# Perceiver kernel on one core: order of the folded queries at the head, and filler matmuls at three places

## The reference

```python
x = x + _L0_xattn_ref(_layernorm(x), ctx_768, Wq, Wk, Wv, Wo, bo)      # 8 heads of 64
x = x + _L0_attn_ref(_layernorm(x), ...)                               # 16 heads of 16, masked
x = x + _L0_ffn_ref(_layernorm(x), ...)                                # 16 experts, top 2, capacity 20 a expert, and a shared one
x = x + _L1_xattn_ref(_layernorm(x), ctx_768, ctx_768, ...)            # 16 heads of 16
x = x + _L1_attn_ref(_layernorm(x), ...)                               # linear attention and a feed-forward part
x = x + _L1_ffn_ref(_layernorm(x), ...)                                # 8 experts, each takes its 32 best tokens
```

```python
q = (x @ Wq).reshape(B, Nq, H, D)
k = (context @ Wk).reshape(B, Nkv, H, D)
v = (context @ Wv).reshape(B, Nkv, H, D)
sim = jnp.einsum('bihd,bjhd->bhij', q, k) * SCALE
attn = jax.nn.softmax(sim, axis=-1)
out = jnp.einsum('bhij,bjhd->bihd', attn, v).reshape(B, Nq, H * D)
return out @ Wo + bo
```

## Time and profile before

| | us |
|---|---|
| median of 3 runs | 1153.56 |
| lowest and highest | 1152.36 and 1153.65 |
| the profiled execution's own time | 1152.36 |
| its span in the profile | 1150.6 |
| TensorE's mean granted clock | 0.984 |
| TensorE busy (matmuls) | 1112.0, 97% of the span |
| VectorE busy | 653.5, 57% |
| ScalarE busy | 665.7, 58% |
| GpSimd busy | 218.8, 19% |

### The profile page before, as it was taken

How to read it: one execution, slowest core, us unless ns; L and a number is a source line. 1 busy time by engine, 2 the same in 40 slices (tenths; PEclk the granted TensorE clock), 3 DMA queues, 4 the chain that set the end, 5 groups by cost and what they waited for, 6 DMA issues and landing times.

```text
span 1150.6 us, 28454 instructions
## 1 busy us (share of the span) xinstructions
PE 1112.0 (97%) x9902; PEld 919.3 (80%) x9902; DVE 653.5 (57%) x1107; ACT 665.7 (58%) x1102; POOL 218.8 (19%) x316
## 2 busy tenths in 40 slices
PE   6999899999999999999987999999999999999998
PEld 4788688888888888888863788888887888888874
DVE  4999654444444444444364688888886444444342
ACT  1888343343433433434231488887888999999631
POOL 0000100000000000000003477777770110000030
PEclk8999899999999999999999999999999999999988
DMA  3544620101110011100445477667665897655191
GB/s 133 136 138 136 248 82 29 35 27 27 29 34 27 27 28 36 27 27 19 169 178 215 136 232 236 219 227 227 225 223 191 307 311 250 199 183 196 63 399 42
DMA packets 63577, 163.28 MB, mean 142 GB/s; under 512 B 6912, under 2 KB 8384, under 8 KB 58368
## 3 DMA queue, kind: packets, MB, share of 16 engines
q1 hardware_dynamic: 54592, 119.06, 32.2%
q0 software_dynamic: 8960, 43.87, 10.0%
HBM read 124.08 MB, written 38.80 MB: 142 GB/s over the span
## 4 chain that ended last, share of the span: by engine, by line
PE 86%; DVE 7%; issue 5%; DMA 1%; DVEq 1%; ACT 1%; POOL 0%; ACTq 0%
PE ps L707 55%; PE ps L957 8%; PE ps L891 8%; PE ps L695 2%; PE ps L742 2%; DVE wide L1456 1%; DVE wide L1464 1%; PE ps L753 1%; PE ps L757 1%; PE ps L754 1%; PE ps L755 1%; PE ps L756 1%; PE ps L1108 1%; PE ps L1279 1%; DMA wa<-ex_in 1%
## 5 line engine op out<-in xcount | busy, mean ns | idle before, releaser
L1526 DVE TENSOR_TENSOR wide<-wide,probs 128x1024 f32<-128x1024 f32 x97 | 118.9, 1226 | 225.3 <-ACT probs L549 224.9
L1456 DVE TENSOR_TENSOR wide<-ps,wide 128x512 f32<-128x512 f32 (+1 forms) x194 | 185.7, 957 | 28.2 <-PE ps L707 23.8
L534 ACT CAST wide<-ps 128x512 bf16<-128x512 f32 x294 | 161.9, 586 | 30.7 <-PE ps L707 25.7
L549 ACT ACTIVATE probs<-ps 128x512 f32<-128x512 f32 x196 | 114.7, 599 | 81.2 <-PE ps L707 81.2
L707 PE MATMUL ps<-q_ha,t_ha 128*128 128x512 f32 x392 | 157.5, 402 | 4.0 <-DVE q_le L1386 3.8
L559 ACT ACTIVATE probs<-ps 128x1024 f32<-128x1024 f32 x132 | 128.0, 1026 | 17.5 <-PE ps L707 15.5
L1464 DVE TENSOR_TENSOR wide<-wide 128x512 bf16<-128x512 bf16 (+1 forms) x194 | 108.0, 557 | 13.0 <-ACT wide L534 2.6
L707 PE MATMUL ps<-q_ab,q_hk 128*128 128x512 f32 x392 | 107.6, 395 | 1.4 <-DVE q_ab L1392 1.3
L707 PEld LDWEIGHTS ps<-q_ha,t_ha 128*128 128x128 f32 x392 | 75.7, 193 | 22.3 <-DVE q_le L1386 4.3
L544 ACT COPY weights_q<-ps 128x512 f32<-128x512 f32 x48 | 28.1, 586 | 106.0 <-PE ps L891 90.0
L1514 DVE COPY v_sb<-wide 128x256 f32<-128x256 f32 x98 | 28.7, 295 | 98.7 <-PE ps L957 97.9
(11 more groups left out here) (421 smaller groups left out, 2400.3 us busy)
## 6 DMA issues: line engine op xcount, KB each, us to landing
raw<-ctx_in SPq DMA_DIRECT2D x147, 256.0 KB, 2.7
k_mem<-q_hk SPq DMA_DIRECT2D x49, 512.0 KB, 3.0
v_mem<-probs SPq DMA_DIRECT2D x49, 256.0 KB, 3.4
wide<-v_mem SPq DMA_DIRECT2D x49, 256.0 KB, 4.0
q_le<-k_mem SPq DMA_DIRECT2D x17, 512.0 KB, 4.3
q_ab<-k_mem SPq DMA_DIRECT2D x16, 512.0 KB, 4.0
q_hk<-k_mem SPq DMA_DIRECT2D x16, 512.0 KB, 4.1
ring<-ex_in POOLq DMA_DIRECT2D x5, 1152.0 KB, 13.3
```

The lines of the kernel that those rows point to most:

```text
L534: act.copy(half16[:, c:c + 512], ps[:, back_bank(layer, q) + u, :]).then_inc(sem(f"half{layer}"), 1)
L549: act.activation(e_keep[GT * slot + j][:, u * 512:(u + 1) * 512], ps[:, s_bank[j][u], :], ACT.Exp).then_inc(sem("exp0"), 1)
L1456: dve.tensor_tensor(r, scores, r, ALU.max).then_inc(sem(f"front{layer}"), 1)
L1526: dve.tensor_tensor(run[:, 0:1024], run[:, 0:1024], e, ALU.add).then_inc(sem("lsum"), 1)
```

## The change

1. The weights' load is cut at another column: the key weights (1284 columns, 657 KB) come alone, with a semaphore of their own (`wk0_loaded`), and value and output weights (2304 columns, 1180 KB) are loaded after the first two context groups. VectorE waits for them after pass 1.
2. The scaling of the queries is gone; the scale is in the mask that the block diagonals are multiplied with. VectorE reads the queries from PSUM for each of the four diagonals and signals each. TensorE starts the first half of the fold after two of them.
3. ScalarE rounds `q_ha` and `q_he` (`keep_queries0`, between its rounding of context groups 0 and 1), VectorE keeps `q_b` and the two remainders, each of which waits for ScalarE's part (`q_high`).
4. Fillers: 3 before the fold and 7 behind it; 7 before the gather of layer 0's experts; in the tail 4 behind each of the first two bias products, 4 in place of the fourth before the scores, and bias products three and four with 2 fillers behind each in place of the ten. In the tail that makes 16 fillers where there were ten.
5. Counts of `q_diag` elsewhere rise by three.

The diff:

```diff
--- before.py
+++ after.py
@@ -285,7 +285,8 @@
             sp.dma_start(cst[:], const_in).then_inc(sem("const_loaded"), 16)
             wk0 = XQ0["wk"]
             sp.dma_start(wa[:, 0:wk0], xq0_in[:, 0:wk0]).then_inc(sem("wq0_loaded"), 16)
-            sp.dma_start(wa[:, wk0:XQ0W], xq0_in[:, wk0:XQ0W]).then_inc(sem("xq0_loaded"), 16)
+            wv0 = XQ0["wva"]
+            sp.dma_start(wa[:, wk0:wv0], xq0_in[:, wk0:wv0]).then_inc(sem("wk0_loaded"), 16)
             def load(layer, g, slot, first):
 
                 if not first:
@@ -333,7 +334,12 @@
 
                 sp.dma_start(kp[slot][ONE, :].bitcast(F32), kp[0][ONE, :].bitcast(F32)).then_inc(sem(f"k_in{slot}"), 16)
 
-            groups(sp, lambda g, slot, first: load(0, g, slot, first))
+            def load_first(g, slot, first):
+                load(0, g, slot, first)
+                if first and slot == 1:
+                    sp.dma_start(wa[:, wv0:XQ0W], xq0_in[:, wv0:XQ0W]).then_inc(sem("xq0_loaded"), 16)
+
+            groups(sp, load_first)
             sp.wait_ge(sem("hi0"), GROUPS)
 
             load_all(0, 0, True)
@@ -352,7 +358,7 @@
             load(1, 3, 1, False)
             store_values(0, 0)
             store_keys(1, 1)
-            sp.wait_ge(sem("q_diag"), 3)
+            sp.wait_ge(sem("q_diag"), 6)
             sp.dma_start(q_mem.rearrange("n r q -> r n q"), qt[0:CB, :].rearrange("r (n q) -> r n q", n=UNITS))\
                 .then_inc(sem("q_out"), 16)
 
@@ -579,6 +585,14 @@
                     act.wait_ge(sem(f"v_out{slot}"), kv_count(slot, g - 2))
                 act.copy(stage[:, slot * 512:(slot + 1) * 512], ps[:, 7, :]).then_inc(sem("staged"), 1)
 
+            def keep_queries0():
+
+                for c in range(2):
+                    act.wait_ge(sem("q_folded"), c + 1)
+                    cs = slice(c * 512, (c + 1) * 512)
+                    act.copy(q_ha[:, cs], ps[:, 1 + 3 * c, :]).then_inc(sem("q_high"), 1)
+                    act.copy(q_he[0:CB + 1, cs], ps[0:CB + 1, 3 + 3 * c, :]).then_inc(sem("q_high"), 1)
+
             def pass1(layer):
                 def body(g, slot, first, last=False):
                     if layer == 1 and not last:
@@ -593,6 +607,7 @@
                             keep_values(g + 1, 1 - slot, first and slot == 0)
                 if layer == 0:
                     round_hi(0, 0, True)
+                    keep_queries0()
                 else:
                     keep_rests(0, 0)
                     keep_values(0, 0, True)
@@ -715,15 +730,17 @@
                         c = XQ0["wq"] + k * inner + b * P
                         last = mm(ps[:, 0, b * P:(b + 1) * P], wa[:, c:c + P], xt[:, k * P:(k + 1) * P], k, DK)
                 last.then_inc(sem("q_psum"), 1)
-                pe.wait_ge(sem("q_diag"), 1)
-                pe.wait_ge(sem("xq0_loaded"), 16)
+                keep_warm(3, 7)
+                pe.wait_ge(sem("wk0_loaded"), 16)
                 for c in range(2):
+                    pe.wait_ge(sem("q_diag"), 2 * c + 2)
                     for part, (o, m) in enumerate(((0, P), (P, P), (2 * P, CB + 1))):
                         for b in range(2 * c, 2 * c + 2):
                             last = mm(ps[0:m, 1 + 3 * c + part, (b % 2) * 256:(b % 2) * 256 + 256],
                                       wa[:, XQ0["wk"] + b * QS + o:XQ0["wk"] + b * QS + o + m],
                                       scr[:, b * 256:(b + 1) * 256], 0, 1)
                     last.then_inc(sem("q_folded"), 1)
+                keep_warm(7, 7)
                 pe.wait_ge(sem("q_chunk"), 2)
 
             def queries1():
@@ -814,7 +831,7 @@
                                 last = mm(o, t_e[slot][0:CB + 1, ks], q_he[0:CB + 1, cs], 1, 2)
                             else:
                                 if first and t == 0 and n % 2 == 0:
-                                    pe.wait_ge(sem("q_diag"), 2 + n // 2)
+                                    pe.wait_ge(sem("q_diag"), 5 + n // 2)
                                 b, w = divmod(n, 2)
                                 last = mm(o, ke[slot][:, b * GK + j * P:b * GK + (j + 1) * P],
                                           (q_la, q_b)[b][:, w * 512:(w + 1) * 512], 0, 1)
@@ -1242,16 +1260,19 @@
                 pe.matmul(ps[:, i, :], own[:, at:at + P], b1, start=True, stop=False, skip_group_check=True)
 
             pe.wait_ge(sem("b1_loaded"), 32)
-            for i in range(3):
+            for i in range(2):
                 bias1(i)
+                keep_warm(4, 4)
             turn_x(7, 6, xn, fill=0, bank=4)
             for k in range(DK):
                 last = mm(ps[:, 6, 0:E1], xt[:, k * P:(k + 1) * P], wlb[:, LB["wr"] + k * E1:LB["wr"] + (k + 1) * E1], k, DK)
             last.then_inc(sem("router"), 1)
-            bias1(3)
+            keep_warm(4, 4)
             pe.wait_ge(sem("scores_r"), 1)
             pe.transpose(ps[0:E1, 6, 128:256], sm[:, 32:32 + E1], ident).then_inc(sem("scores_t"), 1)
-            keep_warm(10, 5)
+            for i in range(2, 4):
+                bias1(i)
+                keep_warm(2, 4)
             pe.wait_ge(sem("picked"), 1)
             pe.transpose(ps[:, 5, 0:E1], sel[:, 2 * P:3 * P], ident[0:E1, 0:E1]).then_inc(sem("scores_t"), 1)
             pe.wait_ge(sem("taken"), 1)
@@ -1368,21 +1389,19 @@
                 dve.wait_ge(sem("const_loaded"), 16)
                 link(dve.tensor_copy(ident16[:], ident))
                 dve.wait_ge(sem("q_psum"), 1)
-                link(dve.tensor_scalar(qt[:], ps[:, 0, :], float(HD[0]) ** -0.5, None, ALU.mult))
                 for b in range(4):
-                    last = dve.tensor_tensor(
+                    dve.tensor_tensor(
                         scr[:, b * 2 * P:(b + 1) * 2 * P].rearrange("p (h q) -> p h q", h=2),
-                        qt[:, b * P:(b + 1) * P].unsqueeze(1).to_broadcast([P, 2, P]),
-                        spread(cst[:, CONST["mask2"]:CONST["mask2"] + 2], P), ALU.mult)
-                last.then_inc(sem("q_diag"), 1)
+                        ps[:, 0, b * P:(b + 1) * P].unsqueeze(1).to_broadcast([P, 2, P]),
+                        spread(cst[:, CONST["mask2"]:CONST["mask2"] + 2], P), ALU.mult).then_inc(sem("q_diag"), 1)
                 for c in range(2):
                     dve.wait_ge(sem("q_folded"), c + 1)
                     b = 1 + 3 * c
                     cs = slice(c * 512, (c + 1) * 512)
-                    dve.tensor_copy(q_ha[:, cs], ps[:, b, :])
                     dve.tensor_copy(q_b[:, cs], ps[:, b + 1, :])
-                    link(dve.tensor_copy(q_he[0:CB + 1, cs], ps[0:CB + 1, b + 2, :]))
+                    dve.wait_ge(sem("q_high"), 2 * c + 1)
                     dve.tensor_tensor(q_la[:, cs], ps[:, b, :], q_ha[:, cs].bitcast(F32), ALU.subtract)
+                    dve.wait_ge(sem("q_high"), 2 * c + 2)
                     dve.tensor_tensor(q_le[0:CB, cs], ps[0:CB, b + 2, :], q_he[0:CB, cs].bitcast(F32), ALU.subtract)\
                        .then_inc(sem("q_chunk"), 1)
 
@@ -1467,6 +1486,7 @@
                 dve.wait_ge(sem(f"run{layer}"), TILES)
                 if layer == 0:
                     va, vb = wa[:, XQ0["wva"]:XQ0["wva"] + 512], wa[:, XQ0["wvb"]:XQ0["wvb"] + 512]
+                    dve.wait_ge(sem("xq0_loaded"), 16)
                     value_his(512, va, vb)
                 for name, bank, at in (("lanes_f", (1, 4)[layer], 0), ("lanes_t", (3, 0)[layer], heads // 2)):
                     dve.wait_ge(sem(name), layer + 1)
@@ -1883,7 +1903,7 @@
     f = np.float32
     return (np.eye(P, dtype=f), (p[:, None] < p[None, :]).astype(f),
             np.where(p[None, :] > p[:, None], f(-1e30), f(0)).astype(f),
-            (p[:, None] // 64 == np.arange(2)[None, :]).astype(f),
+            np.where(p[:, None] // 64 == np.arange(2)[None, :], f(HD[0] ** -0.5), f(0)),
             (p[:, None] // 16 == np.arange(8)[None, :]).astype(f),
             np.broadcast_to(np.arange(E0, dtype=f)[None, :], (P, E0))), (
             (p[:, None] % 4 == np.arange(4)[None, :]).astype(f),
```

## The result

The change took 1147.64 us (median of 5 executions, 1146.38 to 1148.10) beside 1152.91 for the kernel before (1152.36 to 1153.65): a ratio of 0.9949, interval 0.9936 to 0.9962. The direction was right, the size was not. The gain is 5.3 us where 10.6 was forecast, and the time lies 1.6 us above the range's upper end. The profiled execution took 1147.41 us, its span is 1145.6, its mean granted clock 0.988.

A forecast was written before the change was run, and what follows sets the result against it. TensorE, busy in 97% of the span, was taken to lose time waiting or at half clock, at the head through one chain. Head 8.0, gather 1.6 and tail 1.0 sum to 10.6 us: 1152.36 to 1141.8 us, range 1138.2 to 1146.0.

The forecast's parts named there:

- I take **1.0 us** of gain: Tail: 2.6 us won up to the picks' transpose, less a later clock fall; bounds 4.2 gained, 1.5 lost.
- the head's 8.0: Head: 4.75 from an earlier pass 1, 3.05 from its clock, 0.2 from a late load; bounds 3.0 and 8.5.
- the gather's 1.6: Layer 0's gather: seven fillers keep full clock where 3.30 us ran at half, 1.6 us; bounds 0 and 1.7.
- Start of the fold: Head: no scaling pass, diagonals from PSUM at 0.42 us each; fold starts 1.3 us earlier, at 10.1.
- a rival: Head: clock falls once more, price 1.7 us, and the tail brings nothing: 1144.5 us; chance 0.18.
- the forecast 4.75: Head: pass 1 starts at 17.65 instead of 22.39 us, after earlier fold, full clock and shared rounding.
- Fold, rounding, clock of pass 1: Head: fold 5.4 us at full clock, rounding 2.1 us, then pass 1 without half clock, worth 3.05 us.
- 3.25: Start of pass 1: 3.05 us from no half clock and 0.2 us from a late context load.
- the 3.05 us: Start of pass 1: seven fillers fill the rounding, so 6.1 us at half clock cost nothing, 3.05 us.
- Context supply: Pass 1 rival: context loads landing after 3.4 us instead of 2.7 cost 13 us, 1155 us; chance 0.02.
- My remark on the earlier trace: Tail before: TensorE 100% busy with three 16-partition bias products, yet clock 0.50 from 1114.0 to 1124.1 us.

The follow-up runs named there:

- mixed tail: The change with the third bias product replacing four fillers before the router's scores, the fourth between four and five fillers before the picks; 1142.56 us, ratio 0.9929.

## Why the prediction was half right

Two steps failed. The larger is the sum itself: it adds head, gather and tail, and so puts the stages between them at nothing, without a reason; they gave 3.4 us back. The other is the tail's "I take **1.0 us** of gain", which came out as 0.5 us lost. Of the 5.7 us between 10.6 and the 4.9 of the two profiles, these are 3.4 and 1.5; the head's 8.0 came out as 7.1, the gather's 1.6 as 1.7.

**Start of the fold.** Right in its mechanism. The four diagonals from PSUM take 1.42 us, 0.355 each, as much as from SBUF (1.43) and less than the 0.42 I took. So the Trainium skill's advice to copy first (VectorE: DVE Perf Modes, Rules for kernel authors) does not pay here. The key weights were in time. The fold still began at 11.01, not at 10.1, and pass 1 at 18.42, not at 17.65, because the query products took 3.72 us instead of 2.81: I had taken the moment at which the clock first rises from one execution. Over the 20 traces, whose code is the same up to there, they took 2.73 to 3.72, and pass 1 with the new head began between 17.38 and 18.48. That the rise differs from run to run is what the Trainium skill says (TensorE: Matmul & The Clock Gate, Part 1), and these traces show it. I had used it for a rival where it belonged in the sum, as 0 to 1 us. Counted from the end of the query products, pass 1 starts after 8.4 us in all 17 traces of the new head and after 12.9 to 13.3 in the three of the old: 4.5 to 4.8 us for the forecast 4.75.

**Fold, rounding, clock of pass 1.** Right: fold 5.42 (5.4), then 2.0 us to pass 1 (2.1), clock 1.00 to 28.5 and on to 116.6. The half clock's end and the late load were worth 7.1 - 4.0 = 3.1 us (3.25). Head in all 7.1 for 8.0. Of the 3.25 credited to a pass 1 without half clock, though, only 1.5 hang on the head's fillers: without them one stretch of 3.4 us comes back, not two. And the 3.05 us were partly luck of the trace that I read: there the clock was at half for 6.8 us at the start of pass 1, in the two other traces of the old head (the gather's fillers alone, the new tail alone) for 3.4. The three fillers ahead of the fold get no share: it ran at full clock without them.

**Context supply.** This rival did not come: the last maximum lies 7.1 us earlier at 0.933 us a tile as before.

**Gather.** Right: one-hot to the last of the shared expert's products 3.7 us instead of 5.4, 1.7 for 1.6, at full clock:

```profile
593.90:597.40 3.50, 2.93 (x10) 1.84 (x11) 3.06 (x5) 0.00 (x0) 0.00 (x0) 1.00 0.00 0
```

The clock falls there in all 6 traces without these fillers, the one with 28 waits in their place among them, and in none of the 14 with them.

**Tail.** Failed. The first half of its working held: the picks' transpose came 2.2 us earlier behind the first bias product, for 2.6; of the missing 0.4 us, 0.3 lie at its start, where two bias products and eight fillers took 4.2 us and not 3.6 and so held up the transposes of the tokens. The fall of the clock behind it was foreseen too, but it lasted 10.1 us, not 6.1, and cost 2.7, not about 1.6: -0.5 in place of 1.0. In the mean of seven traces each, the change's tail is worth 0.2 us, alone 0 (1.0008). That the mix of the work decides is shown by the mixed tail: two 16-row products close together ahead of the picks against one between nine fillers, 36.7 against 33.2 us, no overlap between the traces. Whether it is the spacing of the products or the number of fillers behind them is not told apart, since the edit changes both. My remark on the earlier trace rows, that such products don't hold the clock, was the right reading, and it spoke against the change's last two, which I priced too low.

**What was not in the sum.** I let everything between the gather and the tail come along unchanged. Layer 1's pass 1 gave 3.3 us back (243.6 against 240.3), and the experts of layer 0 0.8 (31.7 against 30.9 us, 6.8 instead of 3.4 us at half clock). That stretch at the experts lasts 3.4 or 6.8 us in traces with the gather's fillers and in traces without, so the 0.8 is nothing that the change is shown to cause. Of the 3.3 us some 1.0 is the half clock ahead of layer 1's maxima, which comes in 7 of the 20 traces and whose cause stays open; the other 2.3 are the slow alignment. This part isn't the fillers' work but their code: 28 instructions moved the fetch of a 16 KB block onto a store and the context load behind it. Shown are the correlation over 16 traces, both crossings (fillers with the quick alignment twice, waits without fillers with the slow), the store's 4.5 us against 3.0, and the late split, which sorts the alignments in all 20 traces. Not shown is what places a fetch: 28 instructions at the gather moved it 3.2 us, 28 more there and 20 or 32 ahead of a loop did not. Nor was a kernel found that keeps all of the change and has the fetch elsewhere.

The sum as it came, from the table: 7.1 + 0.3 (pass 2) + 1.7 - 0.8 - 3.3 + 0.4 (rest of layer 1) - 0.5 = 4.9 us, the difference of the two profiled executions (1152.36 - 1147.41 = 4.95).

The version with the lowest median is the change with the mixed tail, 1142.56 us (ratio 0.9929 against the change's 0.9949). Four of six kernels with this tail had medians of 1142.6 to 1144.7, the other two, with waits or fillers ahead of pass 2, 1146.7 and 1148.0; the intervals of the ratios overlap that of the change, so that it is faster as a whole is likely, not settled.

## What to carry to other kernels

Sum a change over the stages that it doesn't touch as well: where two engines run in a tight rotation (here VectorE and GpSimd), look for what could push them into another one, and compare group times per stage before and after rather than totals. Fillers are only as good as the mix around them: here the clock fell behind two narrow products put side by side, and the same products spread between fillers cost 3.5 us less in the mean of the traces. Price a term that hangs on when the clock rises or falls from several executions, or give it a range.

## What was unexpected of the hardware

- A code fetch of TensorE (16 KB, 1.0 us on one DMA engine) made a 128 KB store land after 4.5 us instead of 3.0 and held up the 256 KB load behind it by 1.0 us. That one delay of 1 us cost some 2.3 us, since it changed the alignment of two engines for the rest of the 49 groups.
- The same bf16 maximum of 128x1024 takes 0.69 us, or 0.95 when it starts inside a certain one of GpSimd's operations (0.83 in the mean of the stage), and GpSimd's product of 128x256 takes 607 ns or, where it meets such a maximum, 1100.
- VectorE's product of 128x256 costs 0.355 us from PSUM and from SBUF.
- A TensorE wait that is met at once takes 0.106 us: 28 of them 3.0 us.
- TensorE, busy in 10.24 of 10.50 us with fillers and two 16-row products in each half, was at half clock right behind; with those products further apart it was not in four traces of six, and for 3.4 us in the other two.
